# Graph attention on one core: denominators turned by transposes and added by VectorE, logits in another PSUM bank

## What is computed

```python
ft = jnp.einsum('nhd,od->nho', hv, W)
e = jax.nn.leaky_relu(a1[src] + a2[dst], negative_slope=NEG_SLOPE)
w = jnp.exp(e - m[dst])
denom = jax.ops.segment_sum(w, dst, num_segments=n)
alpha = w / jnp.maximum(denom[dst], 1e-16)
agg = jax.ops.segment_sum(alpha[:, :, None] * ft[src], dst, num_segments=n)
res = jnp.einsum('nhd,od->nho', hv, W_res)
out = jax.nn.relu((agg + res).reshape(n, H * DOUT))
```

## Time and profile before

| what | us |
|---|---|
| timed runs, median (lowest to highest of 3) | 1943.1 (1936.69 to 1950.57) |
| the profiled execution, its own time | 1933.66 |
| its span | 1931.8 |
| the stage of the 18 units, from the span's start | 480 to 764 |

### The profile page before, as it was taken

How to read it: one execution, slowest core, us unless ns; L and a number is a source line. 1 busy time by engine, 2 the same in 40 slices (tenths; PEclk the granted TensorE clock), 3 DMA queues, 4 the chain that set the end, 5 groups by cost and what they waited for, 6 DMA issues and landing times.

```text
span 1931.8 us, 24018 instructions
## 1 busy us (share of the span) xinstructions
PE 1793.4 (93%) x7984; PEld 1091.3 (56%) x7985; DVE 720.4 (37%) x1790; ACT 391.6 (20%) x1030; POOL 130.2 (7%) x170
## 2 busy tenths in 40 slices
PE   7999999988999986899988999999999999599995
PEld 4556566433333344566657855555588579465563
DVE  4211322498988887211116211151111124522121
ACT  2341220043112222111013321000211211222121
POOL 0000000000000000111124000000000000022221
PEclk9999999999999998899998999999999999799898
DMA  6003100000001013355546101010010022545575
GB/s 191 1 1 118 57 0 1 31 1 1 32 32 45 30 38 147 131 191 189 191 148 175 39 27 49 0 49 1 1 49 1 0 82 87 210 125 138 163 190 134
DMA packets 53755, 149.56 MB, mean 77 GB/s; under 512 B 9394, under 2 KB 20038, under 8 KB 53157
## 3 DMA queue, kind: packets, MB, share of 16 engines
q1 hardware_dynamic: 34101, 88.97, 13.2%
q0 software_dynamic: 12032, 37.59, 7.7%
q10 hardware_dynamic: 7536, 21.85, 3.2%
HBM read 117.92 MB, written 37.83 MB: 81 GB/s over the span
## 4 chain that ended last, share of the span: by engine, by line
PE 80%; DVE 10%; DMA 4%; issue 3%; DVEq 2%; ACT 0%; POOL 0%; ACTq 0%; SPq 0%; POOLq 0%
PE PS L686 24%; PE PS L1005 10%; PE PS L696 8%; PE PS L1115 5%; PE PS L1135 4%; PE PS L759 4%; PE PS L1087 4%; DVE WRA L1760 4%; PE PS L1073 4%; PE PS L1046 4%; PE PS L914 2%; DMA WS<-in_fW 2%; PE PS L923 2%; PE PS L830 2%; DVE WRB L1760 2%
## 5 line engine op out<-in xcount | busy, mean ns | idle before, releaser
L686 PE MATMUL PS<-WS,XT 128*125 128x384 f32 x960 | 312.4, 487 | 1.4 <-issue 1.4
L686 PEld LDWEIGHTS PS<-WS,XT 128*125 128x125 f32 x960 | 179.9, 188 | 128.9 <-issue 2.6
L1005 PE MATMUL PS<-WS,XGT 128*128 x600 | 199.6, 490 | 0.0
L1005 PEld LDWEIGHTS PS<-WS,XGT 128*128 128x128 f32 x600 | 113.1, 192 | 74.5 <-issue 2.2
L696 PE MATMUL PS<-XT,WS 128*128 128x416 f32 (+1 forms) x432 | 151.2, 512 | 0.0
L1760 DVE SCALAR_TENSOR_TENSOR WRA<-RB,U,AT 125x500 f32<-125x500 f32 (+1 forms) x240 | 140.0, 646 | 3.9 <-ACT AT L1243 1.1
L1894 DVE TENSOR_TENSOR YS<-PS,EBB 128x768 f32<-128x768 f32 x48 | 46.0, 957 | 246.1 <-PE PS L1005 191.5
L696 PEld LDWEIGHTS PS<-XT,WS 128*128 128x128 f32 x432 | 81.6, 189 | 69.2 <-issue 69.2
L1115 PE MATMUL PS<-WS,XGT 128*128 x288 | 104.5, 516 | 10.3 <-DMA WS<-in_fW 9.2
L914 PE MATMUL PS<-WRA,F 125*64 125x500 f32 (+1 forms) x480 | 100.9, 539 | 10.7 <-DVE WRA L1760 10.1
L579 POOL DMA_INDIRECT XG<-xn_rows,IDX x53 | 52.1, 983 | 759.4 <-DVEq L1855 642.8
(11 more groups left out here) (310 smaller groups left out, 2051.1 us busy)
## 6 DMA issues: line engine op xcount, KB each, us to landing
WS<-in_ewT SPq DMA_DIRECT2D x8, 2304.0 KB, 10.6
WS<-in_fW SPq DMA_DIRECT2D x16, 1152.0 KB, 8.3
WS<-in_w SPq DMA_DIRECT2D x5, 2304.0 KB, 10.3
expert_rows<-YS ACTq DMA_DIRECT2D x25, 384.0 KB, 2.3
xn_rows<-XN ACTq DMA_DIRECT2D x20, 336.0 KB
RB<-expert_rows SPq DMA_DIRECT2D x12, 488.3 KB
WS<-in_wp SPq DMA_DIRECT2D x2, 2304.0 KB, 11.9
WS<-in_W SPq DMA_DIRECT2D x2, 2304.0 KB, 8.1
```

What stands on the lines that cost most here:

```text
L686: last = nc.tensor.matmul(ps[0:T, 0:HC], lhsT[:, k, t * T:(t + 1) * T], w[:, k, b * HC:(b + 1) * HC], start=(k == 0), stop=(k == KC - 1))
L1005: last = nc.tensor.matmul(PS[:, 4 + 2 * a + b, 0:HC], XGT[:, a, k, :], WS[:, bass.ds(slot, 1), k * C + b * HC:k * C + (b + 1) * HC].rearra ...
```

## The change

The product with `pick` becomes one transpose for each tile, which fills a whole bank (up to 4 x 128 columns). VectorE reads from it the last column of each quarter of 32: the maximum with TINY over the partial sum v = 0 goes to a new tile RDP, and a new `tensor_tensor` adds v = 1, before the reciprocal. Since bank 5 is full now, the logits of tiles 0 to 7 go to bank 7, column 376, between the transposed rows (columns 0 to 374) and the logit rows (from 384). So `turned_half(t, 0)`, which writes to bank 7, waits for `lg_emptied` of tile t - 1 and no longer for `lr_emptied`. Tiles 8 and 9 have banks 4 and 5. The tile `pick` and the instruction that filled it are gone; the tiles laid out after it up to `rb_base` lie 32 bytes lower.

```diff
-LG_AT = 64
+LG_AT = 3 * T + 1
-    pick = sb("pick", [P, 2])
-    cursor[0] = rb_base = base + 5024 + 4 * 2 * DMAX * 4 + 2 * DMAX * 4 + 4 * P * 4 + 64
+    cursor[0] = rb_base = base + 5024 + 4 * 2 * DMAX * 4 + 2 * DMAX * 4 + 4 * P * 4 + 64 + 32
+    RDP = sb("RDP", [T, 4, 2])
@@ turned_unit
             for i in range(nt):
-                nc.tensor.matmul(PS[0:T, 5, 2 * i:2 * i + 2], UT[:, u % 2, 1, i * T:(i + 1) * T], pick, start=True, stop=True)
+                nc.tensor.transpose(PS[0:T, 5, i * P:(i + 1) * P], UT[:, u % 2, 1, i * T:(i + 1) * T], ident)
@@ turned_half
                 if 0 < t < LATE:
-                    pe.wait_ge(lr_emptied, t)
+                    pe.wait_ge(lg_emptied, t)
@@ logits1
-            nc.tensor.matmul(PS[0:T, 4 if t > LATE else 5, LG_AT + t * NE:LG_AT + (t + 1) * NE], LR[1 if t < LATE else 2][:, t % 2, :], fold, start=True,
+            nc.tensor.matmul(PS[0:T, 7 if t < LATE else t - LATE + 4, LG_AT:LG_AT + NE], LR[1 if t < LATE else 2][:, t % 2, :], fold, start=True,
                              stop=True).then_inc(lg_filled, 1)
@@ VectorE, constants
-        V.tensor_tensor(pick, ident[:, 31:64:32], ident[:, 95:128:32], ALU.add)
@@ denominators
-            V.tensor_scalar(rdn, PS[0:T, 5, 0:2 * nt], TINY, None, ALU.max)
+            parts = PS[0:T, 5, 0:nt * P].rearrange("p (t v j c) -> p v t j c", t=nt, v=2, j=2)[:, :, :, :, P // RG - 1]
+            V.tensor_scalar(RDP[:, 0:nt, :], parts[:, 0], TINY, None, ALU.max)
+            V.drain()
+            V.tensor_tensor(RDN[:, 0:nt, :], parts[:, 1], RDP[:, 0:nt, :], ALU.add)
             V.drain()
             V.reciprocal(rdn, rdn)
@@ bias_logits
-            V.tensor_tensor(LG[:, t, :], PS[0:T, 4 if t > LATE else 5, LG_AT + t * NE:LG_AT + (t + 1) * NE], RBI[:, 0, :],
+            V.tensor_tensor(LG[:, t, :], PS[0:T, 7 if t < LATE else t - LATE + 4, LG_AT:LG_AT + NE], RBI[:, 0, :],
                             ALU.add).then_inc(lg_emptied, 1)
```

## The result

The changed kernel takes 1952.22 us (median of 11 timed runs, 1944.85 to 1960.49), the kernel before 1940.89 us beside it (11 runs); the ratio is 1.006, with a 95% interval of 1.004 to 1.008. So it is slower, by 8 to 16 us, less than 1%. The profiled execution has a span of 1947.1 us, 15.3 more than that of before.

What follows compares the result with a forecast made beforehand. In the stage both engines bound units 1 to 7 in a circle of 16.5 us; TensorE leads in units 10 to 12, VectorE in 14 to 16. Terms 3.69 + 3.1 = 6.8 us on 1943.1 gave 1949.9, range 1936 to 1963.

Steps and rivals of the forecast that it cites:

- The wait: TensorE at `turned_half(t, 0)`, s = 5, waits for VectorE's bias: 1.90 us in units 8 to 10, 1.77 in unit 14.
- What of it shows, unit by unit: Lengthening after slack and savings: 1.07 us each in units 8 and 9, 1.67 in 10, 0.8 in 14 and 15, 1.3 in 16.
- VectorE waits in turn for the first half of L923: After unit 14's wait, VectorE's first weights of the next unit wait 0.6 us for TensorE's delayed L923.
- The added instruction: One more 125x8 VectorE instruction with its drain in the denominators: 0.23 us, bounds 0.16 and 0.27.
- The saving on TensorE: Transposes replacing L859's products: 0.87 - 0.64 = 0.23 us saved per unit of 4 tiles, 0.12 per unit of 2.
- The clock: Waits of this length can lower TensorE's granted clock and need not; the forecast sum has none of it.
- rival C: The clock falls at each of the six waits, some 2 us a time: +18.8 us, 1961.9; chance 0.12.
- the sum of 6.8 us: Stage lengthening: 3.69 us through unit 13 plus 3.1 for units 14 to 17 and the last `turned_unit`.
- Rival A: The forecast: the bias wait shows as worked out, +6.8 us, 1949.9 as the median; chance 0.70.
- B: The bias wait is absorbed by slack: +0.8 us, 1943.9; chance 0.10.
- D: The clock falls at a wait and stays low through a whole unit: +45 us and the 6.8, 1995; chance 0.02.
- E: Tiles moved by 32 bytes change loads or reads elsewhere: 8 us either way, 1942 to 1958; chance 0.06.

Runs made afterwards that it cites:

- e1: Changed kernel with VectorE adding the logits' bias at s = 6, ahead of the denominators, in place of s = 8; 1939.03 us, ratio 1.0007.
- a_after: The changed kernel as it is, run and profiled again beside the kernel before; 1952.13 us, ratio 1.0064.
- e5: Changed kernel with the bias at s = 9 in place of s = 8, behind one more tile of weights; 1960.7 us, ratio 1.0094.
- e10b: Kernel before with the denominators at s = 7 in place of s = 6, the bias left at s = 8; 1932.12 us, ratio 0.9962.
- e2: Changed kernel with RDP put where `pick` lay, so every other tile lies where it lay before; 1948.2 us, ratio 1.004.
- e8: e3 plus one unused 125x8 VectorE instruction with a drain in the denominators; 1952.97 us, ratio 1.0069.
- e3: Kernel before with one line changed: the first half of the transposes waits for `lg_emptied` in place of `lr_emptied`; 1944.31 us, ratio 1.0018.
- e7: Changed kernel with the bias at s = 7 in place of s = 8, one tile of weights less ahead of it; 1935.71 us, ratio 0.9983.

## Why the prediction was right, and where its sizes were off

The forecast was no change beyond 1% and a few us on the slow side, 1949.9 as the median; measured are 1952.22. That these two lie so close is in part luck, as the sum below shows. By its steps:

- *The wait* (1.90 us in units 8 to 10, 1.77 in 14 to 16, behind the denominators and two tiles of weights): right in place and size. Measured 1.93 three times, and 1.83, 1.69 and 2.16. In the working TensorE goes on 3.67 us after `fin_pe`; in the profile of unit 8 it is 621.07 less 617.30, 3.77. e1 shows that it is the cause, and not only that it is there.
- *What of it shows, unit by unit*: right where the clock held. From one `turned_unit` to the next the changed kernel is longer than before by 0.81 in unit 8, 1.54 in unit 10, 0.85 in unit 15 and 1.32 in unit 16; worked out were 1.07, 1.67, 0.8 and 1.3. Units 9 and 14, with a fall of the clock behind the wait, are longer by 2.82 and 1.58, where 1.07 and 0.8 were worked out. The lines of unit 10, before and after:

```profile
654.10 0.93 PE L859 MATMUL PS<-pick,UT 128*125 128x2 f32 x8
...
671.64 0.93 PE L859 MATMUL PS<-pick,UT 128*125 128x2 f32 x8
```

```profile
656.69 0.60 PE L859 MATMUL PS<-ident,UT 128*125 128x128 f32 x4
...
675.77 0.60 PE L859 MATMUL PS<-ident,UT 128*125 128x128 f32 x4
```

- *VectorE waits in turn for the first half of L923* (0.6 us in units 15 to 17): right. The profile has 1.17, 0.73 and 0.73, the first behind a fall of the clock, and 0.93 in unit 9.
- *The added instruction* (0.23 us): 0.24.
- *The saving on TensorE* (0.23 us for a unit of 4 tiles): mis-sized by half, it is 0.43. I took the four transposes of L861 as 0.64 us, from their first load to the next line's, and put four more at that price. But 0.2 of that is the change over to L914, which comes once whatever stands ahead: the first four transposes now take 0.44 and the last four 0.63. So in units 1 to 7 the two don't cancel, and the sign that units 1 to 6 stay at 16.5 us failed (16.28), as did that of 1.28 us for the loads of a unit (1.07). The fourth L914 of unit 3 starts at 527.64 and that of unit 7 at 594.38, where it was 527.35 and 595.23 before: 1.1 us gained over four units. Without the wait the exchange is worth 3.7 us of the stage (e1), where the working had a loss of 0.8.
- *The clock*: the forecast left it out and gave it to rival C, with a chance of 0.12 and 2 us for each of six falls. A fall costs 1.7 us (0.5 of C's price stood for the microsecond before 696, where the window from 692 to 696 lost 0.16). And it isn't six or none: 2 and 5 of 6 in two profiles of the same kernel. The row held against C, 1.96 us of idle time before 593.93 with the clock at 1.00, didn't carry over to another place: that wait brings the clock down in none of the profiles, waits as long before L876 did so behind half.

So the sum of 6.8 us for the stage (measured 5.4 and 10.2) came out near by two errors of opposite sign. The wait with its slack costs about 5 us (stage of the changed kernel less that of e1, each without its lost work: 9.1 - 3.4 = 5.7 and 13.9 - 9.3 = 4.6; the rest of the timed runs of a_after and e1 is 5.9 apart), the clock 3.4 to 9.3 on top, and the exchange gives 3.7 back. Rival A's mechanism is shown, with C's as its companion, and in the timed runs C's part is the larger: of 12.3 us between the means of a_after and before, 8.7 are lost to the clock and 3.6 are the rest, for which A's sum had 6.8. So the time came out beside the forecast by A's wait with C's clock; A alone would have given less than its sum. B (the wait absorbed) is wrong at s = 8 and right at s = 7. D (a low clock through whole units) was not seen even with waits of 3.2 us: each fall lost 1.7 us, but for one of 3.4 behind the wait of unit 15 in e5, and the old one of e10b. E was not seen, within a microsecond or so; the 9.9 us outside 480 to 770 us in the first pair of profiles, which the prediction had named as a sign of being wrong, were scatter.

## What to carry to other kernels

When a result moves to a bank that another engine writes next, ask where the reader of that result stands in its own program: its place in the order, not its length, is what the writer waits for, and a 0.16 us instruction two tiles too late cost 13 us. A wait shorter than the slack behind it is free (0.6 us here in units 8 and 9), so the reader needn't be moved further than that. And where two engines wait for each other once a unit, first look for the wait that closes the circle: doing the denominators one tile later gave more than the cheaper arithmetic did.

## What the runs showed of the hardware

- An idle time of TensorE of 1.7 to 2.2 us between dense products brought the granted clock down from 2.4 to 1.2 GHz behind 12 of 24 waits (changed kernel 2 and 5 of 6, e2 2 of 6, e8 3 of 6), of 1.45 to 1.7 us behind 1 of 6 (e3, a wait of 1.45), of 0.6 to 1.4 us behind none of 6 (e7), and of 2.6 to 3.2 us behind 6 of 6 (e5). The same kernel draws differently each time.
- The length of the idle time isn't all. The 1.75 to 1.76 us ahead of L914 between `turned_unit` of units 12 and 13 (694.85 in the kernel before) brought the clock down in 10 of 11 profiles, and the 1.83 to 1.97 us ahead of L914 in unit 7 (593.93) in none of the 9 that have it. No run here shows why.
- In the timed runs these falls are worth 8.7 us (changed kernel) against 0 (e3), for waits that are longer by 0.2 to 0.7 us. The timed runs of every kernel are spread, those of the kernel before too (1931.20 to 1951.35 us), so the spread isn't the waits' doing alone.
- Back-to-back fp32 transposes of 128x125 take 0.11 us each; an fp32 product of the same stationary tile has two records and takes 0.22, even with a moving operand of two columns.
